# Expert tiles of 112 slots, and every expert product in two 64-column halves of the array

## The chip, the cores and the metric

The kernel runs on one core of one Trainium2 chip. The metric is the device time of one execution in microseconds. The time before is 133.42 us, the median of 3 runs (133.0 to 133.94). Its TensorE has a 128 x 128 array: a product holds a stationary operand in it (its columns become rows of the result) and streams a moving operand through.

## The reference

One layer of a vision tower, in fp32, for 16 images of 96 x 96 x 3: patches, one class token, causal attention with 16 heads, and a mixture of 8 experts with one expert for each token.

```python
h = patches @ W_proj.T + b_proj + pos_emb            # 16 x 36 patches, 256 channels
h = concatenate([cls_tok, h])                        # 16 x 37 = 592 tokens
h = h + attention(layernorm(h))                      # 16 heads of 16, causal
x = layernorm(h).reshape(592, 256)
logits = (x @ w_red) @ (wg / norm(wg)).T             # 8 experts
idx, scores = argmax(softmax(logits)), max(softmax(logits))
y = gelu(x @ w1[idx] + b1[idx]) @ w2[idx] + b2[idx]  # 256 -> 1024 -> 256, one expert per token
out = h + y * scores
```

With the inputs of the reference the eight experts get 112, 62, 70, 54, 60, 78, 75 and 81 tokens.

## The kernel before

The kernel is written engine by engine, with semaphores; nothing reorders it. The tokens lie on the partitions in five tiles of 128 (the last holds 80). Embedding, attention and the router come first, with the load of the first four experts' weights beside them. Each token gets a slot: its expert e and its number within e. GpSimd's `spread` writes the row of each token (its residual, its normalised values, its index and score, 640 words) to that slot in DRAM. Slots that no token fills hold `nil` rows, which SyncE writes early, 128 for each expert.

An expert tile is 128 slots of one expert. For tile t TensorE runs `turn_rows(t)` (two transposes that put the rows' 256 normalised channels on the partitions; ScalarE and VectorE take the copies out of PSUM), `hidden(t)` (first product: for each of 8 slices of 128 hidden channels, two products over the 256 input channels, with `w1s` stationary and the 128 turned slots moving), and `down(t)` (second product: for each of the 8 slices one product with the slots' GELU output `gt` stationary and 256 columns of `w2s` moving). ScalarE's `gelu(t)` stands between them, `rows_turned(t)` and `result(t)` are VectorE's, `scatter(t)` is GpSimd's indirect DMA to `out`. For tiles 0 and 1 no DRAM is passed: `dispatch` on TensorE multiplies the tokens with 0/1 matrices that `places` makes by comparing with `iota`.

The order of the expert stage is written out:

```python
hidden(0)
hidden(1)
down(0)
down(1)
turn_rows(3)
hidden(2)
for t in range(3, E):
    hidden(t)
    if t + 1 < E:
        turn_rows(t + 1)
    down(t - 1)
down(E - 1)
```

`down(1)` holds `turn_rows(2)` in its middle. Weights lie in a ring of four: `load_expert(t)` for t of 4 or more waits until `down(t - 4)` is done. On SyncE's queue the row loads of all tiles (`load_rows`) stand ahead of these loads. After the eight tiles come up to four spare tiles (OVF) for experts with more than 128 tokens; they are skipped when nobody needs them, as here. `tile_position` isn't given in the changed lines: the half of the array follows from where the result starts in PSUM.

## Time and profile before

| | us |
|---|---|
| median of 3 runs | 133.42 |
| the profiled execution | 133.21 |
| its span, first to last instruction | 131.3 |
| TensorE matmul rows busy | 123.1 |
| weight load rows busy | 105.2 |
| VectorE, ScalarE, GpSimd busy | 58.2, 48.2, 41.1 |

PE is TensorE's matmul rows, PEld its weight load rows, DVE is VectorE, ACT ScalarE, POOL GpSimd, SPq SyncE's queue. Matmul rows overlap, since each lasts until its result is out: a group's busy time is the time in which at least one of them runs, and busy time divided by count says more of the pace than the mean of one. In the trace each fp32 product stands as two pairs of load and matmul, each fp32 transpose as one. In "128*64" the first number is the rows and the second the stationary columns.

### The profile page before, as it was taken

To read this page: it belongs to the slowest core of one execution; us is meant where nothing else is said; L and a number is where in the kernel's file an instruction comes from. 1 tells how busy PE (TensorE), PEld (TensorE's weight loads), DVE (VectorE), ACT (ScalarE), POOL (GpSimd) and SP (SyncE) were. 2 spreads that over 40 slices of the span, in tenths; PEclk is the share of its full clock that TensorE was granted. 3 is DMA by queue.
4 is the path that set the end of the run, shared out by engine and by line. 5 is a ranking of instruction groups with operands and counts; after the bars stand their busy time and mean duration, and the time that the engine had idled before them with its cause. 6 is when DMAs were issued, how large, how long until landed. Compare 5 with 4: busy or idle time off the path is not lost.

```text
span 131.3 us, 2718 instructions
## 1 busy us (share of the span) xinstructions
PE 123.1 (94%) x1034; PEld 105.2 (80%) x1034; DVE 58.2 (44%) x179; ACT 48.2 (37%) x143; POOL 41.1 (31%) x52
## 2 busy tenths in 40 slices
PE   5999999999999999999899999999999999999960
PEld 1768897887667777777799998999998989999840
DVE  1231899363986898888957000522102121220210
ACT  0300002383866745662349360066042331506000
POOL 8800034850092193314847500050020202011022
PEclk9999999999999999999999999999999999999999
DMA  4899999159469999999996548999999994000000
GB/s 125 276 394 407 379 411 403 56 176 182 96 138 185 242 362 387 364 386 358 400 352 248 228 124 229 355 405 371 397 362 386 350 377 143 24 0 24 2 28 30
DMA packets 19934, 33.37 MB, mean 254 GB/s; under 512 B 1799, under 2 KB 13704, under 8 KB 19918
## 3 DMA queue, kind: packets, MB, share of 16 engines
q1 hardware_dynamic: 18382, 30.73, 70.8%
q0 software_dynamic: 768, 2.12, 4.3%
q10 hardware_dynamic: 768, 0.31, 0.9%
q8 instruction: 10, 0.16, 0.6%
q14 instruction: 6, 0.05, 0.1%
HBM read 27.75 MB, written 5.84 MB: 256 GB/s over the span
## 4 chain that ended last, share of the span: by engine, by line
PE 68%; DMA 14%; DVE 7%; issue 4%; POOL 3%; SPq 2%; ACT 1%; POOLq 0%
PE ps L793 22%; PE ps L807 19%; PE ps L524 9%; DMA w2s<-v_scratch 5%; DMA early<-embed_in 4%; DMA v_scratch<-hz 4%; PE ps L584 4%; PE ps L591 3%; POOL vbd L1118 2%; PE ps L672 2%; PE ps L685 2%; PE ps L715 2%; PE ps L654 1%; SPq L341 1%; PE ps L776 1%
## 5 line engine op out<-in xcount | busy, mean ns | idle before, releaser
L507 ACT ACTIVATE early<-ps,b1s 128x128 f32<-128x128 f32 x64 | 18.2, 370 | 31.7 <-PE ps L793 31.7
L793 PEld LDWEIGHTS ps<-early,w1s 128*128 128x128 f32 x256 | 29.4, 192 | 0.4 <-issue 0.2
L793 PE MATMUL ps<-early,w1s 128*128 128x128 f32 x256 | 29.6, 275 | 0.0
L807 PE MATMUL ps<-w2s,early 128*128 128x256 f32 x128 | 28.8, 379 | 0.0
L807 PEld LDWEIGHTS ps<-w2s,early 128*128 128x128 f32 x128 | 23.8, 190 | 2.9
L524 PE MATMUL ps<-early 128*128 128x256 f32 x60 | 15.4, 408 | 0.5 <-DMA early<-embed_in 0.5
L524 PEld LDWEIGHTS ps<-early 128*128 128x128 f32 x60 | 11.8, 204 | 3.5 <-DMA early<-embed_in 1.8
L1051 DVE COPY early<-ps 128x256 f32<-128x256 f32 x6 | 2.5, 425 | 25.9 <-PE ps L776 25.9
L1143 POOL DMA_INDIRECT out<-pos,early x4 | 3.9, 970 | 25.7 <-DVE pos L1067 25.3
L1143 POOL DMA_INDIRECT out<-pos,wide x4 | 3.9, 973 | 21.1 <-DVE pos L1067 21.1
L591 PE MATMUL ps<-xnt,wqkv 128*128 128x296 f32 x32 | 9.1, 422 | 0.0
L907 DVE TENSOR_REDUCE negmax<-ps 101x16 f32<-101x592 f32 x8 | 6.2, 772 | 4.6 <-PE ps L617 4.6
L1067 DVE SCALAR_TENSOR_TENSOR pos<-ps,wide,hsum 128x256 f32<-128x256 f32 x4 | 1.9, 483 | 14.1 <-issue 14.1
L401 ACT ACTIVATE xnt<-ps 128x256 f32<-128x256 f32 x5 | 1.7, 380 | 17.0 <-PE ps L571 17.0
L1100 POOL TENSOR_TENSOR rstd<-veps,cf 128x1 f32<-128x1 f32 x5 | 3.2, 632 | 14.4 <-DVE veps L855 14.4
L672 PEld LDWEIGHTS ps<-vbd,probst 111*64 111x64 f32 (+1 forms) x192 | 6.1, 125 | 1.6 <-issue 1.3
L457 ACT ACTIVATE ot<-ps,bv 128x74 f32<-128x74 f32 x16 | 4.3, 323 | 7.8 <-PE ps L679 7.8
L591 PEld LDWEIGHTS ps<-xnt,wqkv 128*128 128x128 f32 x32 | 5.8, 190 | 1.8 <-issue 0.2
L433 ACT ACTIVATE probs<-probs 101x592 f32<-101x592 f32 x8 | 5.6, 697 | 4.3 <-DVE probs L911 4.2
L672 PE MATMUL ps<-vbd,probst 111*64 111x51 f32 (+2 forms) x192 | 6.7, 215 | 0.4
L1118 POOL TENSOR_TENSOR vbd<-w1s,cf 111x512 f32<-111x512 f32 x4 | 4.1, 1066 | 8.0 <-DMA w1s<-v_scratch 8.0
L654 PE MATMUL ps<-cf,probs 101*111 101x101 f32 x48 | 6.1, 264 | 0.2 <-ACT probs L433 0.2
(132 smaller groups left out, 168.1 us busy)
## 6 DMA issues: line engine op xcount, KB each, us to landing
w1s<-w SPq DMA_DIRECT2D x8, 1024.0 KB, 10.7
w2s<-w SPq DMA_DIRECT2D x8, 1024.0 KB, 12.2
slot_scratch<-nil SPq DMA_DIRECT2D x1, 2560.0 KB, 15.1
early<-embed_in SPq DMA_DIRECT2D x5, 448.0 KB, 7.2
early<-slot_scratch SPq DMA_DIRECT2D x4, 320.0 KB, 5.4
wide<-slot_scratch SPq DMA_DIRECT2D x4, 320.0 KB, 6.6
b2s<-b SPq DMA_DIRECT2D x4, 256.0 KB, 8.0
wqkv<-w_qkv SPq DMA_DIRECT2D x1, 768.0 KB, 10.7
```

The source lines that it names most:

```text
L433: nc.scalar.activation(probs[:, u % 2, 0:ALLS], probs[:, u % 2, 0:ALLS], ACT.Exp).then_inc(q["probs_ready"], 1)
L507: nc.scalar.activation(gt[:, t % 2, f, :], ps[:, 2 * (t % 2) + f // 4, (f % 4) * P:(f % 4 + 1) * P], ACT.Gelu, bias=b1t[:, f:f + 1]).then_ ...
L524: return nc.tensor.matmul(ps[:, j, 0:D], emb[:, k, D + j * P:D + (j + 1) * P], emb[:, k, 0:D], start=(k == 0), stop=(k == KE - 1))
L584: m = nc.tensor.matmul(ps[:, VALUES_AT[j], 0:DV], xnt[:, k, j * P:(j + 1) * P], wqkv[:, k, 2 * D:3 * D + E], start=(k == 0), stop=(k == KD ...
L591: m = nc.tensor.matmul(ps[:, QK_BANK[a][n], 0:HALF], wqkv[:, k, col:col + P], xnt[:, k, a * HALF:(a + 1) * HALF], start=(k == 0), stop=(k ...
L654: m = nc.tensor.transpose(ps[0:GS, BP + half, g * ROWS:(g + 1) * ROWS], probs[:, u % 2, at:at + GS], ident[0:ROWS, 0:ROWS])
L672: m = nc.tensor.matmul(ps[a * ROW_B:a * ROW_B + w, o_bank(u), g * GH * VW:g * GH * VW + n], probst[:, u % 2, at:at + w], vbd[:, col:col + ...
L793: m = nc.tensor.matmul(ps[:, 2 * (t % 2) + f // 4, (f % 4) * P:(f % 4 + 1) * P], w1s[:, r, k, f * P:(f + 1) * P], xt[:, t % 2, k, :], star ...
L807: m = nc.tensor.matmul(ps[:, 4 + t % 2, 0:D], gt[:, t % 2, f, :], w2s[:, r, f, :], start=(f == 0), stop=(f == FT - 1))
L907: link(V.tensor_reduce(negmax[:, u % 2, :].rearrange("p (r h) -> p r h", r=2), s3, AX.X, ALU.max, negate=True))
L1118: pool.tensor_tensor(vbd[:, 2 * u * VI:2 * (u + 1) * VI].rearrange("p (h w) -> p h w", w=VW)[:, :, 0:DH], v3[g][:, b0:b0 + 2, :].rearrange ...
L1143: pool.indirect_dma_start(out, bass.IndirectOffsetOnAxis(row_of(t).bitcast(U32)[:, 2 * D:2 * D + 1], 0), yout[:, t % 2, :], None, bounds_c ...
```

## The change

An expert tile has CAP = 112 slots instead of 128. The `nil` rows, the row loads, the moving operand of the first product, the GELUs, the copies and the result shrink with it; the tokens' slots stay 1024 rows apart for each expert. Every product of the expert stage is split by stationary columns. The first product takes the slice of 128 hidden channels as two halves of 64, whose results go to partitions 0 to 63 and 64 to 127. The second takes the 112 slots as 64 and 48. The transposes of `turn_rows` become products with the identity, again in halves of 64 channels. `dispatch` keeps full-array products, with 112 moving columns. The spare tiles are five now. The diff, cut:

```diff
@@ -42,7 +42,9 @@
 HALF_T = -(-HALF // P)
 E, F = 8, 1024
 FT = F // P
-OVF = (T + E * (P - 1)) // P - E
+CAP = 112
+HALVES = ((0, 64), (64, CAP))
+OVF = (T + E * (CAP - 1)) // CAP - E
 RING = 4
 FIRST = D + 2 * P
...
@@ -116,8 +118,8 @@
     putb("ones", 1.0)
     putb("before", p[:, None] < p[None])
     putb("base", np.tile(APART // P * (1 + np.arange(E)), NT)[None])
-    slot = np.arange(ONCHIP * P)
-    iota = (APART * (1 + slot // P) + slot % P).astype(np.float32).reshape(1, ONCHIP * P)
+    slot = np.arange(ONCHIP * CAP)
+    iota = (APART * (1 + slot // CAP) + slot % CAP).astype(np.float32).reshape(1, ONCHIP * CAP)
     return cf, cb.astype(np.dtype("bfloat16")), iota
...
         rows = late(RING * ROW).rearrange("p (r n) -> p r n", r=RING)
-        more = wide[:, NT * ONCHIP * P:NT * ONCHIP * P + (E - RING) * ROW].rearrange("p (r n) -> p r n", r=E - RING)
-        gt = late(2 * FT * P).rearrange("p (b f n) -> p b f n", b=2, f=FT)
-        xt = late(2 * KD * P).rearrange("p (b k n) -> p b k n", b=2, k=KD)
+        more = wide[:, NT * ONCHIP * CAP:NT * ONCHIP * CAP + (E - RING) * ROW].rearrange("p (r n) -> p r n", r=E - RING)
+        gt = late(2 * FT * CAP).rearrange("p (b f n) -> p b f n", b=2, f=FT)
+        xt = late(2 * KD * CAP).rearrange("p (b k n) -> p b k n", b=2, k=KD)
         yout = pos[:, 0:2, :]
         hsum = sb("hsum", [P, 2, D])
 
         def row_of(t):
             r = t % E
-            return rows[:, r, :] if r < RING else more[:, r - RING, :]
+            return rows[0:CAP, r, :] if r < RING else more[0:CAP, r - RING, :]
...
@@ -328,7 +330,7 @@
 
             sp.dma_start(bout[:, :], b_out.partition_broadcast(P)).then_inc(q["loaded_bout"], 16)
             sp.wait_ge(q["nil_ready"], 2)
-            sp.dma_start(of_expert[0:P, :, :], nil[:, :].unsqueeze(1).to_broadcast([P, E, ROW]))\
+            sp.dma_start(of_expert[0:CAP, :, :], nil[0:CAP, :].unsqueeze(1).to_broadcast([CAP, E, ROW]))\
               .then_inc(q["slots_cleared"], 16)
             for g, (j0, j1) in enumerate(((0, HALF_T), (HALF_T, NT))):
...
@@ -351,7 +353,7 @@
             load_expert(RING - 1)
 
             def load_rows(t):
-                sp.dma_start(row_of(t), of_expert[0:P, t, :]).then_inc(gathered[t], 16)
+                sp.dma_start(row_of(t), of_expert[0:CAP, t, :]).then_inc(gathered[t], 16)
 
             sp.wait_ge(q["spread"], 16 * NT)
...
@@ -489,7 +491,7 @@
                 second_rows(j)
             for t in range(ONCHIP):
                 act.wait_ge(q["soon_ps"], KD * t + 1)
-                nc.scalar.activation(xt[:, t, 0, :], ps[:, BX[t][0], 0:P], ACT.Copy).then_inc(q["soon0_ready"], 1)
+                nc.scalar.activation(xt[:, t, 0, :], ps[:, BX[t][0], 0:CAP], ACT.Copy).then_inc(q["soon0_ready"], 1)
             act.wait_ge(q["hot_ready"], 2)
...
@@ -505,7 +507,7 @@
 
                         act.wait_ge(q["hidden_ps"], 2 * t + f // 4 + 1)
                     nc.scalar.activation(gt[:, t % 2, f, :],
-                                         ps[:, 2 * (t % 2) + f // 4, (f % 4) * P:(f % 4 + 1) * P],
+                                         ps[:, 2 * (t % 2) + f // 4, (f % 4) * CAP:(f % 4 + 1) * CAP],
                                          ACT.Gelu, bias=b1t[:, f:f + 1]).then_inc(q["gelu_ready"], 1)
...
@@ -712,8 +714,8 @@
                 pe.wait_ge(q["place32_dve"], j + 1)
                 for t in range(ONCHIP):
                     for k in range(KD):
-                        m = nc.tensor.matmul(ps[:, BX[t][k], 0:P], hz[:, j, D + k * P:D + (k + 1) * P],
-                                             place32[:, j, t * P:(t + 1) * P], start=(j == 0), stop=(j == NT - 1))
+                        m = nc.tensor.matmul(ps[:, BX[t][k], 0:CAP], hz[:, j, D + k * P:D + (k + 1) * P],
+                                             place32[:, j, t * CAP:(t + 1) * CAP], start=(j == 0), stop=(j == NT - 1))
                         if j == NT - 1:
                             m.then_inc(q["soon_ps"], 1)
...
@@ -773,8 +775,10 @@
                 if t >= ONCHIP + 2:
                     pe.wait_ge(q["xt_ready"], t - ONCHIP - 1)
                 for k in range(KD):
-                    m = nc.tensor.transpose(ps[:, 6 + t % 2, k * P:(k + 1) * P],
-                                            row_of(t)[:, D + k * P:D + (k + 1) * P], ident)
+                    for a in range(2):
+                        c = D + k * P + a * ROW_B
+                        m = nc.tensor.matmul(ps[a * ROW_B:(a + 1) * ROW_B, 6 + t % 2, k * CAP:(k + 1) * CAP],
+                                             row_of(t)[:, c:c + ROW_B], ident[0:CAP, 0:CAP], start=True, stop=True)
                 m.then_inc(q["xt_ps"], 1)
 
             def hidden(t):
@@ -790,9 +794,11 @@
                     pe.wait_ge(q["gelu_ready"], FT * (t - 1))
                 for f in range(FT):
                     for k in range(KD):
-                        m = nc.tensor.matmul(ps[:, 2 * (t % 2) + f // 4, (f % 4) * P:(f % 4 + 1) * P],
-                                             w1s[:, r, k, f * P:(f + 1) * P], xt[:, t % 2, k, :],
-                                             start=(k == 0), stop=(k == KD - 1))
+                        for a in range(2):
+                            c = f * P + a * ROW_B
+                            m = nc.tensor.matmul(
+                                ps[a * ROW_B:(a + 1) * ROW_B, 2 * (t % 2) + f // 4, (f % 4) * CAP:(f % 4 + 1) * CAP],
+                                w1s[:, r, k, c:c + ROW_B], xt[:, t % 2, k, :], start=(k == 0), stop=(k == KD - 1))
                     if f % 4 == 3:
                         m.then_inc(q["hidden_ps"], 1)
 
@@ -804,8 +810,9 @@
                     if t == 1 and f == FT // 2:
                         turn_rows(2)
                     pe.wait_ge(q["gelu_ready"], FT * t + f + 1)
-                    m = nc.tensor.matmul(ps[:, 4 + t % 2, 0:D], gt[:, t % 2, f, :], w2s[:, r, f, :],
-                                         start=(f == 0), stop=(f == FT - 1))
+                    for n0, n1 in HALVES:
+                        m = nc.tensor.matmul(ps[n0:n1, 4 + t % 2, 0:D], gt[:, t % 2, f, n0:n1], w2s[:, r, f, :],
+                                             start=(f == 0), stop=(f == FT - 1))
                 m.then_inc(q["y_ps"], 1)
...
             def rows_turned(t):
                 dve.wait_ge(q["xt_ps"], t - ONCHIP + 1)
                 dve.wait_ge(q["hidden_ps"], 2 * (t - 1))
                 V.tensor_copy(xt[:, t % 2, :, :],
-                              ps[:, 6 + t % 2, 0:D].rearrange("p (k n) -> p k n", k=KD))\
+                              ps[:, 6 + t % 2, 0:KD * CAP].rearrange("p (k n) -> p k n", k=KD))\
                     .then_inc(q["xt_ready"], 1)
...
@@ -1057,15 +1064,15 @@
                 b2t = tile_of(t)[2]
                 score = row_of(t)[:, 2 * D + 1:2 * D + 2]
                 dve.wait_ge(gathered[t % E], 16 * (t // E + 1))
-                V.scalar_tensor_tensor(hsum[:, t % 2, :], b2t, score, row_of(t)[:, 0:D],
+                V.scalar_tensor_tensor(hsum[0:CAP, t % 2, :], b2t, score, row_of(t)[:, 0:D],
                                        ALU.mult, ALU.add).then_inc(q["hsum_ready"], 1)
                 dve.wait_ge(q["hsum_ready"], t + 1)
                 dve.wait_ge(q["y_ps"], t + 1)
                 if t >= 2:
 
                     dve.wait_ge(scattered[t % 2], 16 * (t // 2))
-                V.scalar_tensor_tensor(yout[:, t % 2, :], ps[:, 4 + t % 2, 0:D], score,
-                                       hsum[:, t % 2, :], ALU.mult, ALU.add).then_inc(q["y_ready"], 1)
+                V.scalar_tensor_tensor(yout[0:CAP, t % 2, :], ps[0:CAP, 4 + t % 2, 0:D], score,
+                                       hsum[0:CAP, t % 2, :], ALU.mult, ALU.add).then_inc(q["y_ready"], 1)
 
             overflow()
```

TensorE where the experts begin, the end of `dispatch` (L715) and the products of tiles 0 and 1. Before (L793 is `hidden`, L807 `down`, L776 `turn_rows`):

```order
L715 MATMUL ps<-wide,hz 128x128 x8
L793 MATMUL ps<-early,w1s 128x128 x32
L807 MATMUL ps<-w2s,early 128x256 x12
L776 MATMUL ps<-cf,early 128x128 x2
L807 MATMUL ps<-w2s,early 128x256 x4
L776 MATMUL ps<-cf,early 128x128 x2
```

and after (L717 is `dispatch`, L799 `hidden`, L814 `down`):

```order
L717 MATMUL ps<-wide,hz 128x112 x8
L799 MATMUL ps<-early,w1s 64x112 x64
L814 MATMUL ps<-w2s,early 64x256
L814 MATMUL ps<-w2s,early 48x256
L814 MATMUL ps<-w2s,early 64x256
L814 MATMUL ps<-w2s,early 48x256
```

The 32 first products of the two tiles are 64 now, each with 64 stationary and 112 moving columns, and each second product is one of 64 and one of 48 stationary columns.

TensorE in a cycle of the later tiles. Before, from the turning of tile 4 on:

```order
L776 MATMUL ps<-cf,wide 128x128 x2
L807 MATMUL ps<-w2s,early 128x256 x8
L793 MATMUL ps<-early,w1s 128x128 x16
L776 MATMUL ps<-cf,wide 128x128 x2
L807 MATMUL ps<-w2s,early 128x256 x8
L793 MATMUL ps<-early,w1s 128x128 x16
```

and after, from the end of one second product on (L780 is `turn_rows`):

```order
L814 MATMUL ps<-w2s,early 48x256
L814 MATMUL ps<-w2s,early 64x256
L814 MATMUL ps<-w2s,early 48x256
L799 MATMUL ps<-early,w1s 64x112 x32
L780 MATMUL ps<-cf,wide 64x112 x4
L814 MATMUL ps<-w2s,early 64x256
L814 MATMUL ps<-w2s,early 48x256
L814 MATMUL ps<-w2s,early 64x256
L814 MATMUL ps<-w2s,early 48x256
```

No step changed its place; two transposes became four products with the identity, 16 first products became 32, and 8 second products 16.

## Rows read from the trace of the kernel before

**Rows 1.** The page: busy times, granted clock, DMA share, instruction transfers.
```profile
PE 123.1 (94%) x1034; PEld 105.2 (80%) x1034; DVE 58.2 (44%) x179; ACT 48.2 (37%) x143; POOL 41.1 (31%) x52
...
PEclk9999999999999999999999999999999999999999
DMA  4899999159469999999996548999999994000000
...
q8 instruction: 10, 0.16, 0.6%
```

**Rows 2.** The chain that ended last, in order of time: start us, us, what.
```profile
69.08 7.38 PE ps L793 x64
...
81.64 0.22 PE ps L776 x2
...
94.63 3.57 PE ps L793 x32
98.20 0.22 PE ps L776 x2
98.42 3.46 PE ps L807 x16
...
126.94 0.49 DVE pos L1067
```

**Rows 3.** Groups by line and shape, TensorE: busy us, mean ns of one, idle before.
```profile
L793 PE MATMUL ps<-early,w1s 128*128 128x128 f32 x256 | 29.6, 275 | 0.0
L807 PE MATMUL ps<-w2s,early 128*128 128x256 f32 x128 | 28.8, 379 | 0.0
```

**Rows 4.** The chain again, in the stages before the experts.
```profile
18.97 0.45 PE ps L562 x4
...
27.10 2.00 PE ps L591 x8
...
53.45 0.50 PE ps L617 x16
...
54.27 0.58 PE ps L654 x6
```

**Rows 5.** Timeline, 42 to 43.6 us, matmuls, then weight loads: start, us.
```profile
42.11 0.84 PE L672 MATMUL ps<-vbd,probst 111*64 111x51 f32 x24
...
42.08 0.77 PEld L672 LDWEIGHTS ps<-vbd,probst 111*64 111x64 f32 x24 [0.23 <-issue]
```

**Rows 6.** The chain just before the experts.
```profile
62.59 0.88 DVE wide L959 x3
```

**Rows 7.** Timeline of the expert stage: four GELUs, and the first second product.
```profile
74.20 1.14 ACT L507 ACTIVATE early<-ps,b1s 128x128 f32<-128x128 f32 x4 [1.86 <-PE ps L793]
...
76.30 5.34 PE L807 MATMUL ps<-w2s,early 128*128 128x256 f32 x24
```

**Rows 8.** DMAs of w1s and w2s, windows of 82.0, 82.8 and 86.8 us.
```profile
L326 SPq DMA_DIRECT2D w1s<-w x1: 709/709/709, 82.0 to 82.0; - x1
...
DMA to landing us min/median/max: 8.6/8.6/8.6
...
L327 SPq DMA_DIRECT2D w2s<-w x1: 475/475/475, 82.8 to 82.8; - x1
...
DMA to landing us min/median/max: 10.9/10.9/10.9
...
L327 SPq DMA_DIRECT2D w2s<-w x1: 1159/1159/1159, 86.8 to 86.8; - x1
...
DMA to landing us min/median/max: 13.3/13.3/13.3
```

**Rows 9.** The first four row loads.
```profile
L354 SPq DMA_DIRECT2D early<-slot_scratch x4: 340/434/1050, 76.6 to 78.5; - x4
...
DMA to landing us min/median/max: 3.1/5.4/6.3
```

**Rows 10.** A window of the expert stage: busy us, clock, DMA share, GB/s.
```profile
83.00:110.00 27.00, 27.00 (x197) 25.66 (x196) 6.08 (x14) 9.15 (x32) 3.88 (x4) 1.00 1.03 370
```

More of the change, by code:

```diff
@@ L97, in constants @@
     put("revval", ((tok < T)[:, :, None] * (E - np.arange(E))[None, None]).reshape(P, -1))
-    put("thr", P * (1 + np.arange(OVF))[None])
+    put("thr", CAP * (1 + np.arange(OVF))[None])
     put("tri", (np.arange(E)[:, None] >= np.arange(E)[None]).reshape(1, -1))
     put("tilenum", np.arange(OVF)[None])
-    put("tilerow", APART + P * (1 + np.arange(OVF))[None])
+    put("tilerow", APART + CAP * (1 + np.arange(OVF))[None])
     put("tok", tok)
@@ L149, in vit_tower @@
         ident = C("ident")
-        iota = sb("iota", [P, ONCHIP * P])
+        iota = sb("iota", [P, ONCHIP * CAP])
         pos = sb("pos", [P, NT, D])
@@ L186, in vit_tower @@
         kbd = wide[:, :].rearrange("p (c b h s) -> p c b h s", c=KD, b=B, h=HQ)
-        place32 = wide[:, 0:NT * ONCHIP * P].rearrange("p (j s) -> p j s", j=NT)
+        place32 = wide[:, 0:NT * ONCHIP * CAP].rearrange("p (j s) -> p j s", j=NT)
         probs = sb("probs", [ROWS, 2, CH * GS])
@@ L305, in tile_of @@
             b1t = b1s[:, t, :] if t < E else b1o[:, t - E, :]
-            b2t = b2s[:, t, :] if t < E else b2o[:, t - E, :]
+            b2t = b2s[0:CAP, t, :] if t < E else b2o[0:CAP, t - E, :]
             return t % RING, b1t, b2t
@@ L366, in _ @@
                 for i in range(OVF):
-                    sp.dma_start(of_expert[(i + 1) * P:(i + 2) * P, :, :], nil[:, :].unsqueeze(1).to_broadcast([P, E, ROW]))\
+                    sp.dma_start(of_expert[(i + 1) * CAP:(i + 2) * CAP, :, :], nil[0:CAP, :].unsqueeze(1).to_broadcast([CAP, E, ROW]))\
                       .then_inc(q["spill_cleared"], 16)
@@ L372, in _ @@
                     e = sp.value_load(meta[0:1, i:i + 1], min_val=0, max_val=E - 1)
-                    row = sp.value_load(meta[0:1, OVF + i:OVF + i + 1], min_val=0, max_val=(E + 1) * APART - P)
+                    row = sp.value_load(meta[0:1, OVF + i:OVF + i + 1], min_val=0, max_val=(E + 1) * APART - CAP)
                     r = (E + i) % RING
@@ L384, in _ @@
                     sp.wait_ge(scattered[i % 2], 16 * (i // 2 + 1))
-                    sp.dma_start(row_of(E + i), slot_d[bass.ds(row, P), :]).then_inc(gathered[i], 16)
+                    sp.dma_start(row_of(E + i), slot_d[bass.ds(row, CAP), :]).then_inc(gathered[i], 16)
             for b in range(2):
@@ L1021, in _ @@
                 dve.wait_ge(q["soon_ps"], KD * (t + 1))
-                V.tensor_copy(xt[:, t, 1, :], ps[:, BX[t][1], 0:P]).then_inc(q["soon1_ready"], 1)
+                V.tensor_copy(xt[:, t, 1, :], ps[:, BX[t][1], 0:CAP]).then_inc(q["soon1_ready"], 1)
             scores_of(EARLY, NT)
@@ L1043, in overflow @@
                 link(V.scalar_tensor_tensor(orow[:, :], teid[:, :], float(APART), C("tilerow"), ALU.mult, ALU.add))
-                link(V.scalar_tensor_tensor(orow[:, :], obase[:, :], -float(P), orow[:, :], ALU.mult, ALU.add))
-                V.tensor_scalar(meta[:, OVF:2 * OVF], orow[:, :], float((E + 1) * APART - P), None, ALU.min)\
+                link(V.scalar_tensor_tensor(orow[:, :], obase[:, :], -float(CAP), orow[:, :], ALU.mult, ALU.add))
+                V.tensor_scalar(meta[:, OVF:2 * OVF], orow[:, :], float((E + 1) * APART - CAP), None, ALU.min)\
                     .then_inc(q["meta_ready"], 1)
@@ L1142, in scatter @@
                 pool.wait_ge(q["y_ready"], t + 1)
-                pool.indirect_dma_start(out, bass.IndirectOffsetOnAxis(row_of(t).bitcast(U32)[:, 2 * D:2 * D + 1], 0), yout[:, t % 2, :], None,
+                pool.indirect_dma_start(out, bass.IndirectOffsetOnAxis(row_of(t).bitcast(U32)[:, 2 * D:2 * D + 1], 0), yout[0:CAP, t % 2, :], None,
                                         bounds_check=T - 1, oob_is_err=False).then_inc(scattered[t % 2], 16)
```

## The prediction

> **What bounds the kernel now.** I read the page first, for who is busy: TensorE at 94% of the span, its clock at the full level in all forty slices, so at 2.4 GHz [rows 1]. Then the chain that ended last, for what the end hangs on. From 69.1 us to 126.9 us it is TensorE's: a steady cycle of 32 passes of the first expert product, 2 of row turning and 16 of the second product, 3.57 + 0.22 + 3.46 = 7.25 us for each expert, with no wait between; then the last result, its scatter and the end, 4.4 us that this change hardly touches [rows 2]. Every fp32 product is two passes, a load and a matmul each: 8 experts x 16 products of L793 are 256 rows of matmul, 8 x 8 of L807 are 128 [rows 3], while a transpose of L776 is one, 2 in each turn [rows 2].
>
> The question is what sets the pace of a pass. From the chain, 3.57/32 = 111.6 ns for 128 moving columns, 3.46/16 = 216 ns for 256, 0.22/2 = 110 ns for a transpose [rows 2]. Elsewhere in the program: L562 moves only 8 columns and still takes 0.45/4 = 112 ns; all it shares with L793 is a load of 128 stationary columns. L654, 111 stationary and 101 moving, takes 0.58/6 = 97 ns. L591, 128 stationary and 296 moving, 2.00/8 = 250 ns [rows 4]. Two prices fit all of these, and a pass takes the larger: **0.87 ns for each stationary column** (112/128, 97/111) and **0.845 ns for each moving column** (216/256, 250/296). So L793 is paced by its weight loads as much as by its moving rows (0.845 x 128 = 108), and 112 moving rows alone would leave it at 112 ns.
>
> Do halves of the array run side by side? L672 already does two column halves, 64 and 37 wide, on the same 111 rows: 24 matmuls in 0.84 us, of which a single one lasts 0.22, so 0.62 us for 11 steps of either half, 56 ns a step. That is the price of 64 stationary columns alone (0.87 x 64 = 56). In line the two loads would need 0.87 x 101 = 88 ns and the two matmuls 2 x 43 = 86. The loads agree: 24 in 0.77 us [rows 5]. L617 runs four tiles of 64 x 64, 148 moving: 16 matmuls in 0.50 us are four rounds of 125 ns, 0.845 x 148 = 125, so four streams cost no more than one [rows 4].
>
> **The change part by part.**
> First product: 256 matmul rows become 512, in 256 pairs of halves. A pair takes the larger of 0.87 x 64 = 56 and 0.845 x 112 = 95 ns. L654's 97 ns is the nearest measured pass; I take 95, with 98 as the dear end. Saved: 256 x (111.6 - 95) = **4.2 us**, or 3.5 at 98. All of it lies on the chain.
> Second product: halves of 64 and 48 stationary, 256 moving, 216 ns before and after: **0**.
> Row turning: six turns, each 2 transposes of 110 ns before, now 2 products x 2 passes x 2 halves, that is 4 pairs of 95: 0.38 - 0.22 = +0.16 us each, **+1.0 us**. All six stand on the chain [rows 2] and nothing covers them.
> Dispatch (L715, now L717): moving 128 to 112, stationary 128: still 112 ns, 0.
> Vector work ahead of the experts: five comparisons L959 lie on the chain (0.88 for the first 3) and lose 32 of 256 columns, an eighth of some 0.3 us each: -0.15 us [rows 6]. Copies, GELUs and results get shorter beside TensorE: 0 while they are hidden. GELU has 1.14 us of work for every 4 slices against 1.79 us of product before and 16 x 95 = 1.52 after, so it stays hidden; a late GELU at 74.2 is needed by the second product only at 76.3, now at about 75.1 [rows 7]. If that cover failed, one group of four, 1.14 us, would lie open once.
> A fifth spare tile (OVF is 5, was 4) lengthens small vector operations at 70 to 72 us, with nobody behind them before 79: 0.
> **Sum** on TensorE: -4.2 + 1.0 - 0.15 = **-3.35 us**; -2.6 with 98 ns pairs in both terms (-3.5 + 1.05 - 0.15).
>
> What comes late next is data. SyncE loads expert 4 after the row loads: w1 is issued at 82.0 and lands 8.6 later, at 90.6, w2 at 82.8 and 10.9 later, at 93.7 [rows 8]. L793 of expert 4 follows the second product that ends at 94.63 on the chain, so 0.9 us of slack. Before that point the change saves 128 x 16.6 ns = 2.1, less three turns 0.5, plus 0.15: TensorE asks for expert 4 at 92.9. The transfer must come 0.8 us earlier, or TensorE waits. It should: the queue runs at full share (1.03, 370 GB/s from 83 to 110 us [rows 10]), w1 and w2 land 3.1 us apart for 1 MB each, so the eight row loads were through near 90.6 - 2.9 = 87.7, 11.1 us after 76.6 [rows 9]. They now carry 112 of 128 rows: an eighth of 11.1 us is 1.4 us. Expert 4 lands at about 92.3. Expert 5's w2, issued at 86.8 with 13.3 to landing, came at 100.1 [rows 8], wanted one cycle after 94.63, at 101.9, now at 99.7, and lands at about 98.7. Experts 6 and 7 follow at 2 MB/370 GB/s = 5.7 us each against 7.25 us of cycle, so their slack grows. SyncE's own waits: load of expert 4 waits for the second product of expert 0, over before SyncE has issued the row loads; expert 5's wait ends about a microsecond earlier, which helps. The rows themselves (first landing 3.1 us after 76.6, at 79.7 [rows 9], wanted at 81.6 [rows 2], now 80.4) keep 0.7 us.
> I take the full -3.35. The profiled run took 133.21 us (span 131.3, 1.9 around it), the median is 133.42: **forecast 130.1 us**, -2.5%.
>
> A rule against the change. The L672 row shows a load starting while the matmul of the same rows runs: 24 loads end within the 0.84 us of 24 matmuls. The Trainium skill, in "TensorE: Matmul & The Clock Gate", Part 3, The mechanism, says that a load overlaps a running matmul only when the row groups differ, and halves by columns have the same rows. Full-array passes of L793 overlap too, so the trace disagrees.
>
> **Rivals.**
> (a) Expert 4's weights don't come earlier, since their place in the queue and not the rows' bytes sets it. TensorE then resumes at 93.7 instead of 92.9, 0.8 us are lost, perhaps 0.3 more at expert 5: 131.0 us. For it: the slack is 0.9 us. Against it: the share is full. Chance 0.13.
> (b) Loads of the halves take turns in one path. A pair is then 112 ns again in the first product, the turns cost 4 x 112 = 0.45 for 0.22: +1.4 - 0.15, so 134.7 us. The change would not do what it says. Against it: 56 and not 88 ns in L672. Chance 0.05.
> (c) The halves share something that L672's 51 columns are too short to show (the feed of moving rows, or the writes of 256 wide results), and each pair costs more than a pass. This is the slower side: the gain of 3.35 us is spread over 256 + 128 + 24 = 408 pairs, so it is gone at 8 ns more for a pair, and at 11.5 ns the kernel is 1% slower. If a pair cost a quarter more than a pass: 256 x 24 + 128 x 54 + 24 x 24 ns = +13.6, 143.7 us; fully in line, 256 x 95 + 128 x 216 + 24 x 95 = +54, some 184 us. Against it: L617's rounds of 125 ns with four streams. Chance 0.07. The Trainium skill, same page, Part 3, Measured speedup vs the span model, gives 2.38 times for three column tiles of 32, a pack 1.26 times as long as one matmul. By that rule the time would be the 143.7 of the quarter; no row here shows such a loss.
> (d) Loads not hidden behind matmuls, as the rule above would have it: each pair adds 56 ns, 408 x 56 = 22.8 us, 152.9 us. Chance 0.01.
> (e) TensorE executes twice as many instructions in this stretch. Ten instruction transfers stand in the page for the whole program [rows 1]; late ones would cost a few tenths each, up to 1.5 us together, 131.6 us. Against it: L672 goes at 4 instructions (2 loads, 2 matmuls) in 56 ns, the new stretch needs 4 in 95. Chance 0.06.
> (f) Overflow: worked out from the reference, the experts get 112, 62, 70, 54, 60, 78, 75 and 81 tokens. The fullest fits exactly. Were one routed otherwise there, a ninth tile with its clearing, second spread and weights would add over 20 us. The smallest lead of a chosen expert is 0.002 in the logit, far above fp32's error. Chance 0.01.
>
> **Numbers.** Forecast 0.67, for 129.4 to 130.9. With (a) and (e) everything up to 131.9 is faster: 0.86. A gain that shrinks to within 1% (132.1 to 134.7; what a measurement of this kernel can tell from no change): (b) and a mild (c), 0.07. Slower: (c), (d), (f), 0.07. The low end, 129.3, is pairs at 94 ns, with the smaller transfers giving a little more; the high end, 131.9, takes in the 98 ns pairs, (a) and (e), and leaves out some 0.15.
>
> **What would show it.** Right: first product 32 steps in 3.04 us, turns 0.38, second 3.46, cycle 6.9; load and matmul rows in pairs that start within some 20 ns of each other; L814 at 128 steps of 216 ns. Wrong: L799 at 112 a pair (b); L814 above 216 a pair (c); idle TensorE ahead of expert 4 or 5 with its weights as releaser (a); TensorE idle by "issue" (e). What would make the forecast wrong most easily is the price of a pair in the second product, since it is 27.6 us of the time and halves gain nothing there.

## The result: slower, 142.67 us, and the profile after

The changed kernel takes 142.67 us (median of 4 runs, 142.11 to 145.02) against 133.68 for the kernel before on the same chip (4 runs): a ratio of 1.065, interval 1.060 to 1.069. Every kernel here is a few per cent slower in some of its executions, so the ratios compare the undisturbed ones, while the medians are of all. Its profiled execution took 142.53 us, with a span of 140.7, against 133.21 and 131.3.

The page of the changed kernel, first the busy times (unit, us, share, instructions), then the slices and the instruction transfers:
```profile
PE 122.4 (87%) x1454; PEld 105.8 (75%) x1454; DVE 57.9 (41%) x179; ACT 47.4 (34%) x143; POOL 40.8 (29%) x52
...
PEclk9999999999999999999999999999999999999955
DMA  4999995349199999999976299999999900000100
...
q8 instruction: 15, 0.25, 0.7%
```
Beside [rows 1], TensorE is busy about as long as before, yet its share falls from 94 to 87%: the new time is not product time. TensorE's last product ends at 128.5 us; the granted clock stands at half of its full level, 1.2 GHz, in the last two slices, where TensorE has nothing left to do. Instruction transfers are 15 instead of 10.

The chain that ended last, of the changed kernel (start us, us, what), shows where the time is:
```profile
70.29 3.22 PE ps L799 x59
73.52 0.35 issue
73.86 0.42 PE ps L799 x3
74.29 0.32 issue
74.61 0.45 PE ps L799 x4
...
75.77 0.98 issue
76.75 2.94 PE ps L799 x57
79.69 5.27 PE ps L814 x48
...
92.41 1.59 PE ps L799 x28
93.99 0.38 PE ps L780 x8
94.38 3.46 PE ps L814 x32
97.83 3.07 PE ps L799 x64
100.90 0.39 PE ps L780 x8
...
121.62 4.43 PE ps L814 x41
126.06 2.57 issue
128.62 0.50 DVE pos L1074
129.17 0.54 issue
129.71 0.49 POOLq L1164
130.20 0.66 POOL out L1150
```
Set against [rows 2], stage by stage:

| stage | before | after | difference |
|---|---|---|---|
| experts begin | 69.08 | 70.29 | +1.2 |
| first products of tiles 0 and 1 | 7.38 | 9.40 (to 79.69) | +2.0 |
| from there to the first product of tile 2 | 7.35 | 7.68 (to 87.37) | +0.3 |
| first products of tiles 2 and 3 | 7.15 | 6.62 (to 93.99) | -0.5 |
| the four cycles after | 28.98 | 27.63 (to 121.62) | -1.35 |
| last second products, to the last result | 7.0 | 7.0 (to 128.62) | 0 |
| last result to the end of the span | 4.4 | 12.1 | +7.7 |

The sum is +9.4, the difference of the two spans. The steady cycles are as forecast: 3.07 + 0.39 + 3.46 = 6.92 us where 6.9 was written. Two stages are not. In the first products of tiles 0 and 1, 128 rows, that is 64 pairs, of 96 ns a pair would be 6.1 us: 3.3 us are lost at gaps. 1.9 us of them are idle time put down to "issue", that is, TensorE waits for nothing that the profile shows; in the rest a few products go at less than full pace between the gaps. And the end has grown by 7.7 us after all products are done. The 1.2 us ahead of the experts are mostly not the change's: `e3_before_long_spare` below, whose executed products are those of before, begins its experts at 70.50, the kernels with tiles of 112 slots at 69.1 to 70.3 (71.3 in the one with extra products).

What stands at the end is found among TensorE's sequencer instructions. The rows of the line of the spare tiles' condition (`if n > i`), changed kernel (duration ns min/median/max, first and last start):
```profile
L833 PEldq COMPARE_BRANCH  x5: 365/3075/3615, 127.0 to 137.3; - x5
```
The same line of the kernel before:
```profile
L826 PEldq COMPARE_BRANCH  x4: 218/289/2716, 123.7 to 124.7; - x4
```
There are five spare tiles, none of them used, so five branches skip five blocks of code. One takes 0.37 us; the other four take 3.1, 3.6, 2.9 and 3.1 us, one after the other, from 127.5 to 140.4, and the span ends at 140.7. Before, four branches take 0.24, 0.34, 0.22 and 2.72 us and are over at 127.4, beside the last result and its scatter. A page's list of busy engines counts none of this, since branches are not counted as busy.

The last scatter is also late. Its rows, changed kernel:
```profile
L1150 POOL DMA_INDIRECT out<-pos,wide x1: 937/937/937, 129.9 to 129.9; - x1
...
DMA to landing us min/median/max: 4.0/4.0/4.0
```
and of the kernel before:
```profile
L1143 POOL DMA_INDIRECT out<-pos,wide x1: 971/971/971, 128.2 to 128.2; - x1
...
DMA to landing us min/median/max: 2.3/2.3/2.3
```
It costs nothing here, as the jumps outlast it, but it would be 1.7 us of the end if they were gone.

### The profile page after: what moved, and what is told of

Same layout as the page of the kernel before. It is cut to its first block, busy times and chain, and to the rows that moved or that the text cites. A ratio compares the mean times of both kernels' runs of the same rounds, so it can differ in the third digit from the quotient of the medians.

```text
span 140.7 us, 3563 instructions
## 1 busy us (share of the span) xinstructions
PE 122.4 (87%) x1454; PEld 105.8 (75%) x1454; DVE 57.9 (41%) x179; ACT 47.4 (34%) x143; POOL 40.8 (29%) x52
## 4 chain that ended last, share of the span: by engine, by line
PE 60%; DVE 12%; DMA 8%; issue 6%; SPq 4%; ACT 1%; POOL 0%; POOLq 0%; DVEq 0%
PE ps L799 19%; PE ps L814 18%; DMA woutt<-w_out_t 8%; PE ps L593 4%; PE ps L586 3%; PE ps L674 3%; PE ps L656 3%; SPq L316 2%; PE ps L687 2%; DVE negmax L914 2%; PE ps L780 2%; PE ps L717 1%; PE ps L681 1%; DVE wide L901 1%; DVE probs L918 1%
## 5 line engine op out<-in xcount | busy, mean ns | idle before, releaser
L814 PE MATMUL ps<-w2s,early 128*64 128x256 f32 (+1 forms) x256 | 29.4, 379 | 0.0
L799 PE MATMUL ps<-early,w1s 128*64 128x112 f32 x512 | 27.5, 260 | 2.1 <-issue 1.9
L799 PEld LDWEIGHTS ps<-early,w1s 128*64 128x64 f32 x512 | 26.1, 137 | 3.3 <-issue 3.1
L509 ACT ACTIVATE early<-ps,b1s 128x112 f32<-128x112 f32 x64 | 17.4, 355 | 32.9 <-PE ps L799 29.4
L814 PEld LDWEIGHTS ps<-w2s,early 128*48 128x48 f32 (+1 forms) x256 | 26.1, 130 | 0.6
L526 PE MATMUL ps<-early 128*128 128x256 f32 x60 | 15.9, 423 | 0.4 <-DMA early<-embed_in 0.3
L526 PEld LDWEIGHTS ps<-early 128*128 128x128 f32 x60 | 12.5, 214 | 3.3 <-DMA early<-embed_in 1.2
L1058 DVE COPY early<-ps 128x224 f32<-128x224 f32 x6 | 2.3, 390 | 26.9 <-PE ps L780 26.9
L1074 DVE SCALAR_TENSOR_TENSOR pos<-ps,wide,hsum 112x256 f32<-112x256 f32 x4 | 1.9, 484 | 13.7 <-issue 13.7
## 6 DMA issues: line engine op xcount, KB each, us to landing
w2s<-w SPq DMA_DIRECT2D x8, 1024.0 KB, 10.9
wqkv<-w_qkv SPq DMA_DIRECT2D x1, 768.0 KB, 11.4
```

The lines of the kernel that those rows point to most:

```text
L509: nc.scalar.activation(gt[:, t % 2, f, :], ps[:, 2 * (t % 2) + f // 4, (f % 4) * CAP:(f % 4 + 1) * CAP], ACT.Gelu, bias=b1t[:, f:f + 1]).t ...
L526: return nc.tensor.matmul(ps[:, j, 0:D], emb[:, k, D + j * P:D + (j + 1) * P], emb[:, k, 0:D], start=(k == 0), stop=(k == KE - 1))
L799: m = nc.tensor.matmul(ps[a * ROW_B:(a + 1) * ROW_B, 2 * (t % 2) + f // 4, (f % 4) * CAP:(f % 4 + 1) * CAP], w1s[:, r, k, c:c + ROW_B], xt ...
L814: m = nc.tensor.matmul(ps[n0:n1, 4 + t % 2, 0:D], gt[:, t % 2, f, n0:n1], w2s[:, r, f, :], start=(f == 0), stop=(f == FT - 1))
```

## The experiments

Ten of the fifteen have "one jump": the spare tiles' conditions nested, so that an unused first one skips all of the code at once.

### One jump over all spare code, and none at all
`e1_one_jump`, the changed kernel with:
```diff
-            for i in range(OVF):
+            def spare_tiles(i):
                 with pe.If(n > i):
                     turn_rows(E + i)
                     hidden(E + i)
                     down(E + i)
+                    if i + 1 < OVF:
+                        spare_tiles(i + 1)
+
+            spare_tiles(0)
```


> The changed kernel, with TensorE's five tests for spare tiles nested in each other, so that one jump skips all their code. Theory A (the end of the changed kernel is TensorE's sequencer, which takes about 3 us for each jump over the code of a spare tile, 3.1 + 3.6 + 2.9 + 3.1 us after 127.5): one jump of about 3 us is left, it is over near 130.5, and the kernel ends with its last scatter, about 134 to 134.7 of span, 136 to 137 us in all. Rival B (the end waits for something else, the scatters or the drain of the halves, and the branch rows only fill the time): unchanged, 142 to 143 us.

Measured: 135.77 us (134.78 to 136.33), 1.0115 of before (1.004 to 1.019). Of the 9.0 us, 6.9 are gone, with the same executed products. The one branch:
```profile
L833 PEldq COMPARE_BRANCH  x1: 3749/3749/3749, 126.8 to 126.8; - x1
```
It still takes 3.7 us, but is over at 130.5 beside the scatter. So it is the number of long jumps in a row that costs, not the amount of code skipped. The gaps in tiles 0 and 1 stay.

`e2_no_spare_code` leaves the spare tiles' code out on TensorE (they would not be computed; none is used here):
```diff
-            for i in range(OVF):
-                with pe.If(n > i):
-                    turn_rows(E + i)
-                    hidden(E + i)
-                    down(E + i)
```


> The changed kernel without any code for spare tiles on TensorE (it leaves out the products of an expert with more than 112 tokens; these inputs have none). Theory A: the end is that of the last scatter, as with one jump or up to 0.3 us earlier, 136 to 136.7 us. What stays above the 130.1 of the forecast is then not the jumps. Rival B: 142 to 143 us.

Measured: 136.15 us (134.8 to 137.23), 1.011 (1.001 to 1.021). With no jump and the last scatter landing 2.4 us after its start (4.0 in `e1_one_jump`), it should have been below `e1_one_jump`. It wasn't, as its gaps in tiles 0 and 1 were larger. Its chain:
```profile
69.72 2.71 PE ps L799 x52
...
76.27 4.82 PE ps L799 x61
81.10 5.18 PE ps L814 x48
```
From 69.72 to 81.10 are 11.4 us for 64 pairs, 6.1 us. The loss of 3.3 us is thus not a fixed sum: it was 5.2 here.

`e3_before_long_spare` is the kernel before with only the code of the spare tiles, which is never executed, written in halves:
```diff
+                        for n0, n1 in ((0, P),) if t < E else ((0, 64), (64, P)):
```
(and the same in the turning and the second product of a tile t >= E).

> The kernel before, in which only the code of the spare tiles on TensorE is written in halves, and so twice as long; it is never executed, the executed instructions are those of before. Theory A: three of its four jumps, 0.24, 0.34 and 0.22 us before, now take about 3 us each; they start at 123.7 and end near 133 to 136, the kernel takes 136 to 139 us instead of 133.6. Rival B: 133.4 to 133.8 us, code that isn't executed costs nothing.

Measured: 133.71 us (132.62 to 134.56), 0.998 (0.995 to 1.001). The expectation missed: two jumps are long, not four, and they cost nothing. The branches:
```profile
L834 PEldq COMPARE_BRANCH  x4: 219/1660/3030, 125.1 to 131.6; - x4
```
Two of 3 us came where the kernel before had one, which shows that unexecuted code alone makes them. They were over at 131.9, when the last scatter landed too. So the length of the code costs only from the point at which the jumps outlast the last result and its scatter, here 6.8 us after the first branch starts; the two long jumps are just at it, and the changed kernel's four are far beyond it.

### The gaps in tiles 0 and 1
`e4_full_first_two`: one jump, and the first products of tiles 0 and 1 over the full array (the others in halves, so that the later stages are the changed kernel's).
```diff
-                        for a in range(2):
-                            c = f * P + a * ROW_B
+                        for n0, n1 in ((0, P),) if t < 2 else ((0, ROW_B), (ROW_B, P)):
```


> One jump as before, and the first products of tiles 0 and 1 in full-array products with 112 moving columns, half as many instructions there. Theory A2 (the 3 us of gaps in these products, from 73.5 to 76.8 us, come because the instructions arrive too slowly at that time, for all engines, and twice as many are wanted): the two products take about 7.2 us as in the kernel before instead of 9.4, so 2 us less than with one jump alone, 134 to 135 us. Rival B2 (the gaps come from a wait on data or on a semaphore that the halves don't touch): the gaps stay and the products get slower by 1 us, 137 to 138 us.

Measured: 133.84 us (132.32 to 134.46), 0.9967 (0.993 to 1.000). Chain of tiles 0 and 1:
```profile
69.70 7.37 PE ps L798 x64
```
No gap, 7.4 us where the halves took 9.4 to 11.4, and a median just under the 134 to 135 us expected. The gaps are tied to the halves, which take twice the instructions, in this stretch.

`e5_spread_held`: one jump, and GpSimd's spreads held until the first products of tiles 0 and 1 are through (slower as a whole, since expert data comes late).
```diff
+            pool.wait_ge(q["hidden_ps"], 4)
```


> The kernel with one jump, with GpSimd's five spreads held until the first products of tiles 0 and 1 are through. It makes the rows later, so the whole is slower by several us; only the stretch of these two first products is read. Theory A3 (the spreads' many small writes are what slows the supply of instructions, for TensorE, ScalarE and VectorE alike, since each of these stumbles while the spreads run): no gaps in 128 pairs, 6.2 us, and the GELUs follow at once. Rival B3 (twice as many instructions are too many for the supply in any case, or the gaps belong to this place in the code): gaps as before, 9.4 to 9.8 us.

Measured: 142.54 us, one execution. The chain:
```profile
69.80 6.37 PE ps L799 x128
```
All 128 rows (64 pairs; the expectation's "128 pairs" are rows) without a gap, in 6.37 us, 0.23 above 64 x 96 ns. So the halves alone don't make the gaps either: something that goes with the spreads has a part in it.

`e8_shifted_code`: one jump, and 48 tiny products ahead of the embedding, which do nothing but move all later code on by 96 instructions.
```diff
+            for _ in range(48):
+                nc.tensor.matmul(ps[0:32, BZ, 0:8], blank[:, 0:32], blank[:, 0:8], start=True, stop=True)
```


> The kernel with one jump, with 48 tiny bf16 products (32 stationary, 8 moving columns, result unused) added on TensorE before the embedding, so that all later code lies 96 instructions further on in its instruction transfers of 16 KB (256 instructions). If the gaps in tiles 0 and 1 belong to a place within a transfer, they move by some 48 products or vanish; if they belong to the time at which the spreads run, they stay at the same time, from about 2.5 us after the first of these products on.

Measured: 135.43 us, one execution. The first products of tiles 0 and 1 took 71.30 to 77.65, 6.35 us without a gap, although the spreads ran beside them (70.56 to 76.9). The edit moves the later code, and with it the stage starts 1.0 us later than in the changed kernel, products and spreads alike. So, as far as one execution each can tell, both have a part: where the code stands, and what goes on beside it. But the time didn't fall by what the gaps had cost, since now TensorE waited for expert 4's weights, 1.9 us at its weight load:
```profile
83.45 13.28 DMA w2s<-w
96.77 3.29 PE ps L801 x64
```
This is the wait that rival (a) of the prediction names, though longer, hidden behind the gaps until they were gone.

Do the gaps come from a late instruction transfer? `e1_one_jump` has its gaps from 72.4 to 76.2 us. Its DMA queues from 68.4 to 76.3:
```profile
q0 software_dynamic: 349, 1.45, 48.4%
q1 hardware_dynamic: 787, 0.80, 31.3%
```
No instruction transfer is among them. The next one (q8, 16 KB) lies between 76.3 and 77 us, when TensorE has already been at full pace from 76.21 on. In `e5_spread_held`, with the same code on TensorE, it stands at 73.1. In both, TensorE has then done some 65 to 70 of the 128 rows. So here the transfer follows TensorE's progress; it could explain the stop only if its request had waited unseen. TensorE's instructions are not the only thing that is late, either. ScalarE in the changed kernel:
```profile
74.69 1.09 ACT L509 ACTIVATE early<-ps,b1s 128x112 f32<-128x112 f32 x4 [2.25 <-remote]
```
This first GELU waits for the first 32 rows of the first product, and 59 rows are through by 73.52. The signal from TensorE came late too, which late instructions for TensorE alone would not explain.

### What each form of the product is worth
`e6_cap_only`: 112 slots, one jump, everything over the full array and the rows turned by transposes.
```diff
-                    for n0, n1 in HALVES:
-                        m = nc.tensor.matmul(ps[n0:n1, 4 + t % 2, 0:D], gt[:, t % 2, f, n0:n1], w2s[:, r, f, :],
+                    m = nc.tensor.matmul(ps[0:CAP, 4 + t % 2, 0:D], gt[:, t % 2, f, :], w2s[:, r, f, :],
```


> Tiles of 112 slots alone: all expert products full-array, the turning by transposes, one jump. By the price of 0.87 ns for each stationary column the first product stays at 112 ns a step and only 0.15 us of comparisons are saved: 133.2 to 133.8 us, as before. If moving 112 instead of 128 columns were what saves, it would be 256 x 14 ns = 3.6 us less, 130 us.

Measured: 133.29 us (133.11 to 134.79), 1.0003 (0.997 to 1.004). First product 3.57 for 32, second 3.46: as expected, 112 slots alone do nothing. A pass with 112 moving columns keeps the 112 ns of one with 128, as the prediction's price by stationary columns has it.

`e7_late_first_products`: as `e6_cap_only`, with halves in the first products of tiles 2 to 7 alone.
```diff
+                        for n0, n1 in ((0, ROW_B), (ROW_B, P)) if 2 <= t < E else ((0, P),):
```


> Halves only where they save: in the first products of tiles 2 to 7. The second products, the turning (transposes again) and tiles 0 and 1 are full-array, one jump. Six times 32 steps of 96 instead of 112 ns are 3.0 us less, with 0.15 of comparisons: 130.3 us if a change between halves and full array costs nothing. With 0.1 to 0.2 us for each of some 13 changes 131.6 to 133 us.

Measured: 132.95 us (131.97 to 134.22), 0.994 (0.992 to 0.997). Its chain, one cycle:
```profile
101.38 3.22 PE ps L796 x64
104.60 0.34 PE ps L778 x2
104.94 3.46 PE ps L810 x16
```
The cycle is 7.02, where 3.07 + 0.20 + 3.46 = 6.73 was to be had. A first product that follows a full-array one costs 3.22 instead of 3.07 us, and two transposes behind halves 0.34 instead of 0.20: each change of form costs 0.15 us, twice in a cycle. The median is in the range expected with such changes. The changed kernel pays 0.39 for its turning in halves and no change of form: 6.92, the cheaper one.

### The order of the transfers
`e9_weights_first` (as `e7_late_first_products`) and `e11_before_weights_first` (the kernel before) issue expert 4's weights ahead of the row loads of tiles 4 to 7; so does `e10_halves_from_tile2`, which has halves everywhere from the first product of tile 2 on (the rows of tiles 2 and 3 are turned by transposes).
```diff
-            for t in (*range(ONCHIP, RING), *range(ONCHIP), *range(RING, E)):
+            for t in (*range(ONCHIP, RING), *range(ONCHIP)):
                 load_rows(t)
+            load_expert(RING)
             for t in range(RING, E):
+                load_rows(t)
+            for t in range(RING + 1, E):
                 load_expert(t)
```


> Halves in the first products of tiles 2 to 7 alone, as before, and SyncE issues the weights of expert 4 ahead of the row loads of tiles 4 to 7. Theory W (the queue's order sets when expert 4's weights land, at 94.25 us in the run with halves in the first products, just as TensorE asks): they land some 3 to 4 us earlier, near 90.5, TensorE doesn't ask before 94.2, so the gain is at most the 0.07 us by which that tile's first product was longer: 132.5 to 133 us. If TensorE's clock or its own steps set the start, the same.

> Weights of expert 4 first; tiles 0 and 1 and the turning of tiles 2 and 3 in full array, from the first product of tile 2 on everything in halves, one change between the forms; spare tiles' code in full array, one jump. No change of form within a cycle: 6.91 instead of 7.02 us, 6.14 instead of 6.28 for tiles 2 and 3, together 0.7 us less than with halves in the first products alone: 132.2 us. If the instruction transfer of the jump falls 1.3 to 1.8 us after a scatter's start again, the last scatter lands 1.5 us later: 133.7 us.

> The kernel before with the weights of expert 4 ahead of the row loads of tiles 4 to 7. There the weights land 0.9 us before they are wanted, so nothing should change: 133.3 to 133.9 us. If other transfers suffer (the rows of tile 4 late), up to 1 us slower.

Measured: 134.37 (132.78 to 139.09, ratio 1.000, 0.996 to 1.004), 135.68 (132.33 to 139.3, 6 runs, too scattered for a ratio) and 133.98 us (133.02 to 136.04, ratio 0.9996, 0.996 to 1.003). The first two missed; the third came out as its second case had it, the rows of tile 4 late. The wait moved from the weights to these rows. Before a turning stands, in the chain of `e10_halves_from_tile2`:
```profile
80.93 10.16 DMA wide<-slot_scratch
91.14 0.60 PE ps L787 x8
```
TensorE's weight load waited 1.3 us there, and 1.1 in `e11_before_weights_first`.

`e12_full_two_no_spare`: `e4_full_first_two` without the spare tiles' code on TensorE (left out as in `e2_no_spare_code`).

> The kernel with full-array first products in tiles 0 and 1 and halves elsewhere, now without code for spare tiles on TensorE (it leaves out the products of experts with more than 112 tokens; these inputs have none). Theory S (a 16 KB instruction transfer that starts 1.3 to 1.8 us after the start of a scatter delays its landing from 2.4 to 3.8 us): no jump, no transfer, the last scatter lands 2.4 us after its start, 132.3 to 132.5 us instead of 133.8. Rival (112-row scatters behind halved products land late by themselves): 133.8 us.

Measured: 132.38 us (131.52 to 133.53), 0.989 (0.986 to 0.992), as expected. The last scatter lands 2.4 us after its start, and 3.8 in `e4_full_first_two`, which is nearly all of the 1.5 us between the two. What is left is the wait for expert 4's weights, in its chain:
```profile
81.23 13.79 DMA w2s<-w
95.07 3.29 PE ps L798 x64
```
The weight load waits 1.2 us for them. w2 takes 13.8 us to land, issued at 81.2, where the kernel before needs 10.9 from 82.8 [rows 8].

`e13_halves_jump_early`: halves from tile 2 on as in `e10_halves_from_tile2`, tile 7's second product over the full array, one jump, and the rows of tile 4 ahead of expert 4's weights, those of 5 to 7 behind them.
```diff
-            for t in (*range(ONCHIP, RING), *range(ONCHIP), *range(RING, E)):
+            for t in (*range(ONCHIP, RING), *range(ONCHIP), RING):
                 load_rows(t)
-            for t in range(RING, E):
+            load_expert(RING)
+            for t in range(RING + 1, E):
+                load_rows(t)
+            for t in range(RING + 1, E):
                 load_expert(t)
...
-                    for n0, n1 in HALVES:
+                    for n0, n1 in HALVES if 2 <= t < E - 1 else ((0, CAP),):
```


> As with halves from tile 2 on, but SyncE issues the rows of tile 4 before, the rows of tiles 5 to 7 after the weights of expert 4, and the second product of tile 7 is full-array. Theory D (what TensorE waits for at expert 4 is the queue's order alone): no wait for rows or weights at 91 to 95 us. Theory S: with the last second product in half as many instructions TensorE's sequencer comes to the jump some 3.4 us earlier, the instruction transfers start before the last two scatters or with them and these land 2.4 us after their start. Together 131.0 to 131.5 us; with the wait still there 132.3, with late scatters 132.7.

Measured: 131.81 us (131.36 to 133.94), 0.985 (0.981 to 0.988). It computes all that the reference asks for, and is 1.5% faster than the kernel before. Its chain:
```profile
69.28 7.37 PE ps L805 x64
...
94.07 3.07 PE ps L805 x64
97.14 0.39 PE ps L787 x8
97.52 3.46 PE ps L820 x32
...
125.04 0.50 DVE pos L1084
```
No gap and no wait; the last result stands at 125.04 instead of 126.94 [rows 2]. Its jump, 3.4 us from 122.1, is over before the last scatter, which lands 2.4 us after its start.

`e14_first_products_rows4` and `e15_bound` are `e7_late_first_products` and `e12_full_two_no_spare` with that order of transfers.

> Halves in the first products of tiles 2 to 7 alone, with the rows of tile 4, then the weights of expert 4, then the other rows. The wait of 3 us for the rows of tile 4 that the other order brought is gone; the first product of tile 4 starts without a wait: 132.4 to 132.9 us, the cycle stays at 7.02 us with its two changes of form.

> The kernel without spare code on TensorE (it leaves out the products of experts with more than 112 tokens; these inputs have none), full-array first products in tiles 0 and 1, halves elsewhere, with the rows of tile 4, the weights of expert 4, the other rows. Theory D: the wait of 1.17 us at the first product of tile 4 goes, 131.1 to 131.4 us; this is the sum of the forecast, 130.1, plus 1.1 for the two full-array first products. If transfers only change places and something else waits, 132.4.

Measured: 132.22 us (131.9 to 133.89), 0.987 (0.985 to 0.989), and 132.04 (131.69 to 132.84), 0.986 (0.983 to 0.989). The first came 0.2 us below its range. The second missed its first case by 0.6 us and came nearer to its other one, "if transfers only change places": the wait for expert 4 is gone, and one of 1.2 us for expert 5 is there:
```profile
85.93 16.44 DMA w2s<-w
102.41 3.29 PE ps L801 x64
```
The transfers have only changed places. With the DMA share full in this stretch [rows 10], the transfers are a second bound, right behind TensorE: here an order gave one tile its data in time at the cost of another's.

## Why the prediction was wrong

It forecast 130.1 us, -3.35, and the time rose by 9.0. Step by step:

- **Price of a pair, first product**: 95 ns forecast, 3.07/32 = 96 measured. Right, and with it the two prices that it rests on. The Trainium skill, "TensorE: Matmul & The Clock Gate", Part 3, The mechanism, would have no load overlap a matmul on the same rows. The trace disagrees: 96 ns are the 95 of the moving columns alone, without the 56 of a load. The same page, Part 3, Measured speedup vs the span model, gives 2.38 times for three column tiles, from which the prediction worked out a pack 1.26 times as long as one matmul. No such loss appeared with two.
- **Second product**: 0 forecast. Right, to the digit. The rows of both halves, by line and shape, in the changed kernel:
```profile
L814 PE MATMUL ps<-w2s,early 128*64 128x256 f32 x128 | 28.8, 379 | 0.0
L814 PE MATMUL ps<-w2s,early 128*48 128x256 f32 x128 | 28.8, 379 | 0.0
```
Each half is busy 28.8 us in all, as the full array was [rows 3], and the 16 pairs of a tile take 3.46 us. Rivals (b), (c) and (d) are refuted by these rows and the 96 ns.
- **Turning**: 0.38 forecast, 0.38 to 0.39 measured. Right.
- **The cycle**: 6.9 forecast, 6.92 measured. From 93.99 to 121.62 the full gain is there, 1.35 us, and 0.5 more in tiles 2 and 3, where 1.0 was due and 0.5 is lost around a gap at 92.3.
- **Vector work**: -0.15 forecast. The first three comparisons take 0.83 us instead of 0.88 [rows 6], so it is less than half of that, and the start of the experts varies by more.
- **"A fifth spare tile ... with nobody behind them: 0"**: this is the step that failed. The prediction looked at the vector operations that the spare tile lengthens, and not at TensorE's own code for it. Spare tiles are 50 loads with their matmuls each before and 104 after, and there are five instead of four: some 400 instructions to be skipped became 1040. The four long jumps cost 6.9 us (`e1_one_jump`). With this the step "the last result, its scatter and the end, 4.4 us that this change hardly touches" fell too; the end was 12.1.
- **Rival (e)**, late instructions "up to 1.5 us together", named the place, TensorE idle by "issue", and the wrong size: 3.3 us in tiles 0 and 1 and 0.5 later, and 5.2 in `e2_no_spare_code`. Whether its means, late transfers, is right isn't shown. Its argument against, that L672 goes faster still, is true of a stretch without such gaps, which is not this one. A sign stood in the trace of before: ScalarE's wait of 1.86 us [rows 7], with TensorE named as releaser, ends at 74.20, though the 32 rows that it waits for are through at about 72.7 (32 x 111.6 ns after 69.08). So a signal was some 1.5 us late in this stretch already. The prediction took it for a late GELU, hidden behind the products, and didn't ask why it was late.
- **Expert 4's weights at 92.3**: they come no earlier. This couldn't be seen in the changed kernel, since TensorE itself was late; once it isn't, it waits 1.2 us (`e12_full_two_no_spare`). The bytes saved on the rows did not bring w2 forward, which took 13.8 us where it had taken 10.9. Rival (a) named it at 0.8 to 1.1 us, at a chance of 0.13, too low.
- **Rival (f)**: no spare tile was used. Right.

The sum can be closed roughly by the medians, though some neighbours in this row differ in more than one thing (the last one also turns the rows of tiles 2 and 3 by transposes): the changed kernel at 142.67; without the jumps 135.77; with full-array first products in tiles 0 and 1 instead of gaps 133.84; without the late scatter 132.38; without the wait for expert 4, by order and an early jump, 131.81. Of the remaining 1.7 us to the forecast 1.6 have a name: the gain of tiles 0 and 1 in halves, 2 x 0.5 = 1.0, which `e13_halves_jump_early` gives up, 0.45 by which the kernel before itself was slower beside it (133.87 against 133.42), and a change of form of 0.15.

Open is what exactly stops TensorE at 72 to 77 us. Shown is that full-array products don't have the gaps (`e4_full_first_two`). Holding the spreads (`e5_spread_held`) or shifting the code (`e8_shifted_code`) each removed them too, in one execution each. That a late instruction transfer is the means is not shown, and the queues of `e1_one_jump` speak against its simple form. Whether a shift of the code together with the new order would give the halves' 1.0 us in tiles 0 and 1 as well wasn't tried.

## What to carry to other kernels

Count the instructions that a change adds to code that is not executed, and look at the sequencer's branches beside the busy engines: several skipped blocks in a row at a kernel's end are several jumps, one nested condition is one. If a change doubles the instruction rate of an engine, look for a stretch of the trace in which a signal or an instruction is late already: here ScalarE's late start stood in the trace of before. And when the engine that bounds the kernel gets faster by a microsecond, read who is next: here a transfer with 0.9 us of slack, which took a new order of the queue to keep off the chain.

## What the runs showed of the hardware that was not expected

- A branch over code takes 0.22 to 0.37 us, or about 3 (2.7 to 3.9 in the runs here). In the changed kernel instruction transfers stand beside them. DMA from 125 us to the end, busy share in 40 slices, and the instruction queue:
```profile
DMA  0000000610000002500000001000000010000000
...
q8 instruction: 4, 0.07, 1.8%
```
The 2 and 5 at the 16th and 17th slice hold the last scatter too; the lone ones at 134.8 and 138 us are instruction transfers, some 0.6 us into a jump each. One jump over all of the spare code takes little longer than one over a fifth of it (3.75 us against 2.9 to 3.6).
- The last scatter of GpSimd lands 2.3 to 2.5 us after its start or 3.5 to 4.0. It was late in the six kernels where an instruction transfer began 1.3 to 1.9 us after it (the changed kernel, `e1_one_jump`, `e4_full_first_two`, `e5_spread_held`, `e8_shifted_code`, `e10_halves_from_tile2`). It was not late where the transfer came together with it or well apart from it (among them the kernel before, `e3_before_long_spare` and `e13_halves_jump_early`), or not at all (`e2_no_spare_code`, `e12_full_two_no_spare`, `e15_bound`). This is a pattern over these runs; no run moved the transfer alone.
- A change between full-array products and halves costs 0.15 us each way (3.22 against 3.07 and 0.34 against 0.20 in `e7_late_first_products`).
- Two halves of 64 and 48 columns, each moving 256, run at 216 ns for a pair, exactly the price of one full pass.
